# State space kernel and film weights moved into the expert blocks, weights of the last stage loaded by round, logits in another PSUM bank

## What is computed

```python
x = x + _L0_attn_ref(_layernorm(x), L0_attn_W)                      # window attention
x = x + _L0_xattn_ref(_layernorm(x), ctx_768, mask, W_q, W_k, ...)  # cross attention, 8 heads
x = x + _L0_ffn_ref(_layernorm(x), router_w, router_b, W1, b1, W2, b2)   # 8 experts, top 1
x = x + _L1_attn_ref(_layernorm(x), ...)                            # RWKV time mixing, channel mixing
x = x + _L1_xattn_ref(_layernorm(x), ctx_768, ...)                  # top-k cross attention, film, state space layer
x = x + _L1_ffn_ref(_layernorm(x), weights, scale, bias)            # signs of weights times scale
```

```python
dtA = dt[:, None] * A;  dC = C * (jnp.exp(dtA) - 1.0) / A
powers = jnp.exp(dtA[:, :, None] * jnp.arange(L))
K = 2.0 * jnp.einsum('dn,dnl->dl', dC, powers).real      # the state space kernel, 256 channels x 256 steps
scale_in, shift_in = jnp.split(c_t @ W_film_in + b_film_in, 2, axis=-1)   # c_t = attention @ (x_vision @ Wv)
```

## Time and profile before

| | us |
|---|---|
| median of 3 runs | 2089.95 |
| the 3 runs | 2089.79 to 2095.91 |
| the profiled execution | 2093.25 |
| its span in the trace | 2091.5 |

### The profile page before, as it was taken

How to read it: one execution, slowest core, us unless ns; L and a number is a source line. 1 busy time by engine, 2 the same in 40 slices (tenths; PEclk the granted TensorE clock), 3 DMA queues, 4 the chain that set the end, 5 groups by cost and what they waited for, 6 DMA issues and landing times.

```text
span 2091.5 us, 26470 instructions
## 1 busy us (share of the span) xinstructions
PE 1754.7 (84%) x8210; PEld 1360.3 (65%) x8210; DVE 1263.8 (60%) x3880; ACT 862.1 (41%) x1672; POOL 603.5 (29%) x984
## 2 busy tenths in 40 slices
PE   6899999980699999718357899999999999999965
PEld 4677777760466666508346687777787778877744
DVE  3566666651233333292246688888888888887551
ACT  2444444430111111100166566666776766664431
POOL 1111111115101000000334345554544544444221
PEclk9899999985799999955578899999999999999987
DMA  8000000008433333260100000000000000000000
GB/s 253 1 1 1 1 1 1 1 1 328 149 110 113 108 107 106 77 182 1 25 11 6 6 6 11 11 11 6 11 11 11 11 11 1 6 6 6 6 6 10
DMA packets 80751, 90.42 MB, mean 43 GB/s; under 512 B 19092, under 2 KB 69477, under 8 KB 80615
## 3 DMA queue, kind: packets, MB, share of 16 engines
q1 hardware_dynamic: 71927, 75.23, 11.9%
q0 software_dynamic: 3072, 8.39, 1.2%
q10 hardware_dynamic: 5616, 5.11, 0.7%
HBM read 69.84 MB, written 18.87 MB: 42 GB/s over the span
## 4 chain that ended last, share of the span: by engine, by line
PE 33%; DVE 13%; ACT 2%; POOL 2%; issue 1%; POOLq 0%; ACTq 0%
PE E_pY L2191 5%; PE E_pK L2082 5%; PE E_pU L2181 3%; PE E_pK L2041 3%; PE E_pY L2029 3%; PE E_pS L2144 3%; PE E_pY L2162 3%; DVE E_ex L1560 2%; PE E_pU L2153 2%; DVE E_wk L1628 2%; DVE E_m L1621 1%; PE E_pY L2041 1%; PE E_pT L2023 1%; DVE E_num L1567 1%; PE E_pY L2092 1%
## 5 line engine op out<-in xcount | busy, mean ns | idle before, releaser
L946 ACT ACTIVATE F_uT<-F_puT 128x1024 f32<-128x1024 f32 x39 | 39.9, 1023 | 297.6 <-PE F_puT L985 297.6
L976 PE MATMUL F_pu<-C_W,F_hT 128*128 x312 | 144.1, 605 | 0.3 <-issue 0.3
L994 PE MATMUL F_py<-C_W,F_uT 128*128 x624 | 141.3, 380 | 1.2 <-ACT F_uT L946 1.2
L1382 POOL TENSOR_SCALAR E_var<-E_mv 128x2 f32<-128x2 f32 x80 | 35.0, 438 | 356.0 <-DVE E_mv L1497 355.7
L994 PEld LDWEIGHTS F_py<-C_W,F_uT 128*128 128x128 f32 x624 | 115.9, 191 | 15.8 <-issue 1.9
L2092 PE MATMUL E_pY<-E_Wcv,E_hid 128*128 128x256 f32 x512 | 118.7, 387 | 3.3 <-issue 3.3
L2181 PE MATMUL E_pU<-E_xT,E_W 128*128 128x256 f32 x512 | 117.4, 385 | 2.3 <-ACT E_xT L1930 2.3
L2191 PE MATMUL E_pY<-E_W,E_hid 128*128 128x256 f32 x512 | 118.1, 380 | 0.0
L2082 PE MATMUL E_pK<-E_cmix,E_Wck 128*128 128x256 f32 x512 | 116.7, 382 | 1.3 <-ACT E_hid L1871 1.3
L2092 PEld LDWEIGHTS E_pY<-E_Wcv,E_hid 128*128 128x128 f32 x512 | 96.3, 193 | 27.5 <-issue 15.6
L905 DVE TENSOR_TENSOR F_u<-F_pu,F_b 128x1024 f32<-128x1024 f32 x39 | 47.8, 1225 | 109.5 <-DMA F_b<-in_L_ffn_b 93.9
(11 more groups left out here) (422 smaller groups left out, 4484.6 us busy)
## 6 DMA issues: line engine op xcount, KB each, us to landing
F_b<-in_L_ffn_b SPq DMA_DIRECT2D x39, 512.0 KB, 4.5
C_W<-in_L_ffn_W SPq DMA_DIRECT2D x16, 1024.0 KB, 14.6
sorted_x<-zero SPq DMA_DIRECT2D x1, 4992.0 KB, 19.7
F_xs<-sorted_x SPq DMA_DIRECT2D x39, 128.0 KB, 2.4
F_b<-in_L_ffn_b SPq DMA_DIRECT2D x39, 128.0 KB, 4.3
sorted_y<-F_y ACTq DMA_DIRECT2D x39, 128.0 KB, 2.6
out<-E_tB SPq DMA_DIRECT2D x16, 256.0 KB, 2.1
X<-in_x SPq DMA_DIRECT2D x3, 1024.0 KB, 11.8
```

The source lines that it names most:

```text
L976: last = nc.tensor.matmul(p_u[:, f, :], hT[:, i % 2, kb, :], W1[:, bass.ds(e, 1), kb, f * 512:(f + 1) * 512], start=kb == 0, stop=kb == KD ...
L994: last = nc.tensor.matmul(p_y[:, 0:D], uT[:, f, :], W2[:, bass.ds(e, 1), f, :], start=f == 0, stop=f == FB - 1)
```

## The change

`ssm_spectrum` is gone. Its work is cut into slices that stand inside the expert blocks. DVE calls prepare(i) at the end of block i; powers are built in four parts of a quarter of the groups each, in five slices a part (blocks 7 to 26). PE's small matmuls (`kernel`) follow second(i) in blocks 12, 17, 22 and 27 and alternate between the halves of the rows; film follows second(2) and second(3), the spectrum second(32). The slices use the memory of X and of Wkvr. Results go to memory (`folded_film`, `folded_row`, `spectrum`) and are loaded in stage E. SP issues the loads between block loads, and asks for the biases of block i+1 in loop i, ahead of load_xs. In stage E the weights have semaphores by the round that needs them; the sign weights are prepared there at n == 3. In the attention stage the router logits go to p_turn.

```diff
 def choose(i):
-    ve.tensor_tensor(lg[:], p_out[:, 0:2 * E].rearrange("p (t e) -> p t e", t=2),
+    ve.tensor_tensor(lg[:], p_turn[:, 0, 0:2 * E].rearrange("p (t e) -> p t e", t=2),
                      rb[:].unsqueeze(1).to_broadcast([P, 2, E]), ALU.add).then_inc(r["lg"], 1)
 def project(i):
-    past(pe, r["lg"], i - 2)
     past(pe, b["x"], i - 1)
 def logits(i):
     pe.wait_ge(r["hT"], i + 1)
-    past(pe, b["x"], min(i + 1, B - 1))
-    past(pe, r["lg"], i - 1)
     for t in range(2):
         for kb in range(KD):
-            last = te.matmul(p_out[:, t * E:(t + 1) * E], hTR[:, kb, t * P:(t + 1) * P], rw[:, kb, :],
+            last = te.matmul(p_turn[:, 0, t * E:(t + 1) * E], hTR[:, kb, t * P:(t + 1) * P], rw[:, kb, :],
 def turn_B(i):
-    past(pe, r["hT"], i - 3)
+    past(pe, r["lg"], i - 3)
...
 # expert_blocks, SP
+            for i in range(3):
+                load_xs(sp, i)
+            load_biases(0)
+            for i in range(BLOCKS):
+                if i + 1 < BLOCKS:
+                    load_biases(i + 1)
                 if i + 3 < BLOCKS:
                     load_xs(sp, i + 3)
+                if i == 1:
+                    load_film()
+                if i == 2:
+                    load_kernel()
+                if i == 6:
+                    store_film()
+                if i in (12, 14, 16):
+                    load_columns(COLUMNS[4 * (i // 2 - 6):4 * (i // 2 - 6) + 4])
+                if i == 18:
+                    load_last_columns()
+                if i == 20:
+                    load_ahead()
+                if i == 30:
+                    turn_kernel()
+                if i == 35:
+                    store_spectrum()
...
 # expert_blocks, DVE, at the end of each block
+            def prepare(i):
+                part, stage = divmod(i - 7, 5)
+                if i == 2:
+                    fold_row()
+                elif i == 3:
+                    angles()
+                elif i == 4:
+                    fold_film()
+                elif i == 5:
+                    first_power()
+                elif i == 6:
+                    weight()
+                if 0 <= part < 4:
+                    if stage == 0:
+                        short_powers(part)
+                    elif stage == 1:
+                        eighth_power(part)
+                    elif stage == 2:
+                        long_powers(part, 2)
+                        square()
+                        long_powers(part, 4)
+                        square()
+                    elif stage == 3:
+                        long_powers(part, 8)
+                        square()
+                    else:
+                        last_power(part)
+                if i in (14, 19, 24, 28):
+                    keep_kernel((14, 19, 24, 28).index(i))
+                if i == 31:
+                    add_skip()
+                if i == 33:
+                    keep_spectrum()
...
                 residual(i)
                 output(i)
+                prepare(i)
...
 # expert_blocks, ACT, in its loop
+                if i == 3:
+                    step_size()
+                    keep_film(0)
+                if i == 4:
+                    keep_film(1)
+                    first_power()
...
 # expert_blocks, PE
+            def kernel(part):
+                pe.wait_ge(c[f"gp{part}"], 1)
+                pe.wait_ge(c["copied"], 2)
+                if part >= 2:
+                    pe.wait_ge(c["ks"], 4 * (part - 1))
+                for g in range(GC):
+                    for half in range(2):
+                        rows = slice(N * half, N * half + N)
+                        for r in range(2):
+                            last = nc.tensor.matmul(p_k[:, half, part % 2, g].rearrange("p q c -> p (q c)"),
+                                                    gp[rows, r, g].rearrange("p q a -> p (q a)"),
+                                                    pw[part % 2][rows, r, g, :, 0:NC], start=r == 0, stop=r == 1)
+                last.then_inc(c[f"kp{part}"], 1)
...
                 second(i)
-def ssm_spectrum(nc, args, k, w, fourier, C, load):
...
+                if i in (2, 3):
+                    film(i - 2)
+                if i in (12, 17, 22, 27):
+                    kernel((i - 12) // 5)
+                if i == 32:
+                    spectrum_product()
...
 # mixing_and_state_space, SP: 14 matrices, 4 rows, the folded weights and the spectrum, then the stores of out
+            load(Wo, "L1_attn_Wo", "first")
...
+            sp.dma_start(w["Wvf"][:], folded_film).then_inc(lw["second"], 16)
+            sp.dma_start(w["VW"][77:78, :], folded_row).then_inc(lw["second"], 16)
+            sp.dma_start(fourier["spec"][:], spectrum_in).then_inc(lw["third"], 16)
...
 # DVE
+            def sign_and_scale():
+                sign = w["sign"][:]
+                dve.wait_ge(lw["rows"], 16 * (len(ROWS) + 2))
+                chained(v.tensor_scalar(sign, sign, 0.0, 2.0, ALU.is_ge, ALU.mult))
...
+                if n == 3:
+                    sign_and_scale()
+                    dve.wait_ge(lw["third"], 80)
...
 # PE
-            pe.wait_ge(lw["weights"], 16 * 14)
             turn_1(-1, 0)
+            pe.wait_ge(lw["kvr"], 48)
...
+                if n == 2:
+                    pe.wait_ge(lw["second"], 32)
+                if n == 3:
+                    pe.wait_ge(lw["third"], 80)
+                if n == 4:
+                    pe.wait_ge(f["sign"], 1)
...
+                if n == 0:
+                    pe.wait_ge(lw["first"], 16 * 8)
```

More of the change, by code:

```diff
@@ new lines, in load_kernel @@
+            def load_kernel():
+                for half in range(2):
+                    rows = slice(N * half, N * half + N)
+                    cols = slice(P * half, P * half + P)
+                    for n in ("A_re", "A_im", "C_re", "C_im"):
+                        sp.dma_start(m[n.replace("_", "")][rows, :], args["L1_xattn_" + n][:, cols]).then_inc(c["load"], 16)
+                    sp.dma_start(m["ldt"][rows, :],
+                                 args["L1_xattn_log_dt"][cols].partition_broadcast(N)).then_inc(c["load"], 16)
@@ L918, in output, with step, gq, fold_row @@
                 ve.tensor_tensor(y[:, i % 2, :], p_y[:, 0:D], xs[:, i % XB, :], ALU.add).then_inc(s["y"], 1)
+            steps = 0
+            def step(instruction):
+                nonlocal steps
+                steps += 1
+                instruction.then_inc(c["step"], 1)
+                dve.wait_ge(c["step"], steps)
+            def gq(x, part):
+                return x.rearrange("p (q g) -> p g q", g=G4)[:, GC * part:GC * part + GC]
+            def fold_row():
+                dve.wait_ge(c["film"], 16 * 9)
+                step(ve.tensor_scalar(row, row, gate[0:1, 0:1], None, ALU.mult))
+                for j in range(2):
+                    last = ve.tensor_scalar(row[:, j * F2:j * F2 + D], row[:, j * F2:j * F2 + D], 1.0, None, ALU.add)
+                step(last)
+                step(ve.tensor_tensor(folded[0:1, 0, :], row[:, 0:D], b_in[0:1, :], ALU.mult))
+                step(ve.tensor_tensor(row[:, D:F2], row[:, D:F2], folded[0:1, 0, :], ALU.add))
+                ve.tensor_tensor(row[:, 0:D], row[:, 0:D], g_in[0:1, :], ALU.mult).then_inc(c["row"], 1)
@@ new lines, in short_powers @@
+            def short_powers(part):
+                z = pw[part % 2]
+                if part == 0:
+                    dve.wait_ge(c["out"], 32)
+                if part >= 2:
+                    dve.wait_ge(c[f"kp{part - 2}"], 1)
+                ve.memset(z[:, 0, :, :, 0], 1.0)
+                ve.memset(z[:, 1, :, :, 0], 0.0)
+                ve.tensor_copy(z[:, 0, :, :, 1], gq(m["ar"], part))
+                step(ve.tensor_copy(z[:, 1, :, :, 1], gq(m["ai"], part)))
+                for have in (1, 2):
+                    product(z[:, :, :, :, have + 1:2 * have + 1], z[:, :, :, :, 1:have + 1], z[:, :, :, :, have], have)
@@ new lines, in square, with long_powers, eighth_power @@
+            def square():
+                product(t4[:, 0:2, :, :, 15:16], base.unsqueeze(4), base, 1)
+                step(ve.tensor_copy(base.unsqueeze(4), t4[:, 0:2, :, :, 15:16]))
+            def long_powers(part, have):
+                product(gp[:, :, :, :, have:2 * have], gp[:, :, :, :, 0:have], base, have)
+            def eighth_power(part):
+                z = pw[part % 2]
+                product(z[:, :, :, :, 5:9], z[:, :, :, :, 1:5], z[:, :, :, :, 4], 4)
+                if part:
+                    dve.wait_ge(c[f"kp{part - 1}"], 1)
+                for half, n in enumerate(("mag", "cos")):
+                    last = ve.scalar_tensor_tensor(out=gp[:, half, :, :, 0], in0=gq(m[n], part), scalar=2.0,
+                                                   in1=gq(m["a2"], part), op0=ALU.mult, op1=ALU.mult)
+                step(last)
+                step(ve.tensor_copy(base, z[:, :, :, :, NC]))
+                long_powers(part, 1)
```

(16 more changed lines are left out.)

440 lines of the change are left out of this document (207 added, 233 removed).

## The result

The changed kernel takes **1937.71 us** (median of 4 runs, 1935.89 to 1940.07), against 2090.2 for the kernel before in 4 runs: ratio 0.9265, 95% interval 0.9246 to 0.9284. The profiled execution took 1936.92 us, its span is 1935.2. The forecast was 1970, its range ended at 1950: the direction was right, and the gain is a quarter larger than forecast.

A forecast was written before the change was run, and what follows sets the result against it. Prediction: PE bounds the expert blocks, with gaps from bias waits; a chain of engines working singly bounds stage K. Terms summed to -120.2 from 2093.25, giving 1973.0, or 1970 us for the median; range 1950 to 1996.

The forecast's parts named there:

- stage K: Stretch from its first load to stage E's first instruction, where nothing of other stages runs, goes entirely: -142.0 us.
- waits for b1: Expert blocks: DVE's add_b1 no longer waits for the bias, which is loaded a block earlier: -19.4 us.
- SP's new issues: Expert blocks: SP's added loads, stores and a wait eat the period of some blocks: +2 us, between 0 and 6.
- film and spectrum: PE's added records in the expert blocks, paid in full: film 7.2 us, spectrum 3.6 us.
- small matmuls with the clock: Four slices in the expert blocks at 8.1 us each, clock loss included: +32.4 us, between 18 and 60.
- DVE over its slack: Blocks 14, 19 and 24: copy-out on top of DVE's slice exceeds the slack by 1 us: +3, between 0 and 12.
- attention: Logits no longer wait for DVE to clear p_out; 0.7 us a round in 13 rounds: -9, between -4 and -15.5.
- stage E and the way into it: First rows up to 2.8 us later beside weight loads, plus sign weights in round 3: +2 us, between 0 and 8.
- the first step: Small-matmul slices in the blocks: 5.6 us, between 4.5 and 6.8, plus 1.6 after and 0.9 within for the clock.
- the second step: Attention's logits: of PE's 1.19 us idle a round, 0.7 is gained, since ACT's hB is late next: -9 us.
- The forecast's rival on the clock: Each small-matmul slice and its block run at 1.2 GHz, 21.5 us instead of 8.1: +54, so 2024; chance 0.08.
- The range's high end: Small matmuls at the lower level all through, up 28, or 19 with the biases: 1996 us.

The follow-up runs named there:

- halves_strict: The changed kernel with the row halves alternating at every small matmul instead of every second; 1939.19 us, ratio 0.9285 to the kernel before.
- halves_apart: The changed kernel with one half of the rows after the other within each slice of small matmuls; 1960.39 us, ratio 0.9382 to the kernel before.
- wait_filled: The kernel before with two extra, unused sets of transposes in PE's idle time ahead of the logits, no wait removed; 2074.45 us, ratio 0.9939.
- dve_more: The changed kernel with five more DVE operations of 256 elements at the end of blocks 2 to 33; 1969.10 us, ratio 0.9429 to the kernel before.
- alternate_in_K: The kernel before with one loop order changed in stage K, its small matmuls alternating row halves by twos; 2066.02 us, ratio 0.9885.

## Why the forecast was too high

Against the profiled executions, 2093.25 and 1936.92, the difference is -156.3 where -120.2 was forecast, 36.1 more. The median misses by less, 32.3: the forecast took 3.3 off for it, and this execution lies 0.8 under it.

| term | forecast | measured |
|---|---|---|
| stage K | -142.0 | -142.0 |
| waits for b1 | -19.4 | -19.8 |
| SP's new issues | +2 | 0 |
| film and spectrum | +10.8 | +10.3 |
| small matmuls with the clock | +32.4 | +17.0 (4 x 3.81, one fall of 1.75) |
| DVE over its slack | +3 | +3.6 (3 x 1.01, and 0.6 in small ones) |
| attention | -9 | -23.2 |
| stage E and the way into it | +2 | -2.3 |

**Right:** the structure. Stage K went by its full length, the biases by what the periods had shown (19.8 for 19.4), film and the spectrum cost the length of their records, the copies exceeded DVE's slack three times by 1.0. All of this came from differences of two starts in one timeline and needed no judgement. No rival came true.

**Wrong, the first step: "I take the middle, 5.6, since only every second switch is there", and behind it "I expect each slice to end at the lower level: 1.6 after it, 0.9 within it".** 15.4 us of the 36. Switching every second time gives all the overlap that switching every time gives (halves_strict adds nothing): 3.78 a slice. That the switches are fewer was no reason to go up. Attention's scores at 0.070 a record were the nearer row, and even they have more columns (77 for 32). The other row, 6.8 a slice at full clock, was right, but for the order by halves: halves_apart has 0.104 a record there. As for the clock, stage K showed that such matmuls don't *bring* it up; that was read as if they took it down. In slices of 3.8 us the clock fell in 11 of 28, and in one of the four here. The Trainium skill, page "TensorEngine Tiling (Array Packing)", section Key Properties, with its tiles on different rows that load and multiply in parallel, gave the estimate of 3.4 for a slice and would have been nearer; the traces agree with it (0.112 to 0.056 at full clock, 0.210 to 0.106 at the lower level). With 17.0 the term came out even below its low end, 18.

**Wrong, the second step: attention, "0.7 a round and not 1.2, in 13 rounds: -9".** 14.2 us. The rounds gave 0.86, for the reason given: hB became the next late thing. Missing was the clock. The table by stage showed 0.92 for attention, and I passed over it; by rounds it would have shown that some took 23.47 and others of the same kind 25.96, with a clock of 0.50 in 178 to 182 us. The 12 rounds from 126 us went from 305.2 to 286.0: 10.3 for the waits and 8.9 for the clock; the way from the last hB to R_pin went from 46.5 to 41.3 as well. Of that way no run tells the clock and the waits apart. wait_filled shows the clock's part in the whole stage, 11.4 us.

The forecast's rival on the clock looked for it in the blocks and made it a loss. The Trainium skill, page "TensorE: Matmul & The Clock Gate", section "HAM oscillation", on kernels whose bursts between waits start at the lower level, is about waits of 3 to 5 us. The waits of 3.86 us in dve_more fit it. Attention's are 1.19 us, so the page would not have foretold these falls; and in dve_more the clock stayed up behind seven waits of 0.7 to 2.2 us. The falls that mattered were in the other stage, and the change took them away.

**Wrong, small:** stage E was to be 2 longer by gathers beside the loads. They do land later (5.6 us for 2.8), but the first transposes come 15.2 us after the stage's first instruction in both kernels, and the stage is 2.8 shorter. All of it lies in rounds 0 to 4, where the clock comes up at other places (the eight records of `E_pK` ahead of round 4 take 3.78 us before and 1.99 after). Why was not tried. SP's new issues cost nothing that shows.

The range's high end has a slip besides: 28 over 1970 is 1998, not 1996. The range missed because its low end took both errors for rare together ("down: 14 if the small matmuls overlap and hold the clock"), and held attention to the 15.5 of the waits, with nothing for the clock.

## What to carry to other kernels

Read the granted clock of every stage round by round before costing a wait there: here rounds of the same work differed by up to 2.5 us, and a wait of 1.19 us in each cost its own length and, in five of 12 rounds, 0.9 to 2.5 us more by the clock. Removing the wait gave both back, filling it gave the clock back. Put float32 matmuls that use half the rows in alternating order from the start, at every switch or every second: it halved them at either clock here. If such work has to stand between wide matmuls, keep each piece short: here the clock fell in every piece of 8 us, in 11 of 28 of 3.8 us and in 1 of 16 of 2 us, though the pieces of 2 us gained nothing in the end. The vector engine's slices belong in the slack that the periods show, which was about 5 us in a period of 8.

## What the runs showed of the hardware

- 64-row float32 matmuls with 32 columns, from start to start of a record: 0.112 us at 2.4 GHz and 0.210 at 1.2 GHz if one half of the rows follows the other (halves_apart, before), 0.056 and 0.106 if the halves alternate (after, alternate_in_K). Alternating at each matmul gave the same as at every second (3.76 and 3.78 us a slice).
- PE busy without a break is no guarantee for the clock: 27.5 us of narrow matmuls stayed at 0.50 (alternate_in_K), as the 54.0 did before.
- Idle time of 1.19 us a round, filled with transposes of no use, made the attention stage 11.4 us shorter; the granted clock of 12 rounds went from 0.95 to 1.00 (wait_filled).
- In the expert blocks a wait of 3.86 us of PE was followed by 1.5 to 1.8 us of loss by the clock in each of three cases, seven of 0.7 to 2.2 us by none (dve_more). In attention, waits of 1.19 us went with falls in five of 12 rounds (before).
